# The sum B11 + B12 of one weight matrix stands further down in VectorE's program

## The reference

```python
x_not = jnp.take(field_vectors, not_idx, axis=1)
t = jnp.tanh(jax.nn.relu(x_not @ Wn1 + bn1) @ Wn2 + bn2)
iv = field_vectors.at[:, not_idx, :].set(t)

def pair_fuse(pairs, W1, b1, W2, b2):
    v = jnp.concatenate([jnp.take(iv, pairs[:, 0], axis=1), jnp.take(iv, pairs[:, 1], axis=1)], axis=-1)
    return jax.nn.relu(v @ W1 + b1) @ W2 + b2
and_out = pair_fuse(and_pairs, Wa1, ba1, Wa2, ba2)
or_out = pair_fuse(or_pairs, Wo1, bo1, Wo2, bo2)
...
h = jnp.concatenate([z, dense_ctx], axis=1)
h = jnp.maximum(h @ W_top1 + b_top1, 0.0)
h = jnp.maximum(h @ W_top2 + b_top2, 0.0)
y = h @ W_top3
```

## Time and profile before

| | us |
|---|---|
| three runs | 534.53, 537.44, 537.46 |
| median | 537.44 |
| the profiled execution | 535.43 |
| its span | 533.6 |
| TensorE busy in the span | 527.0 |
| VectorE, ScalarE, GpSimd busy | 360.9, 250.4, 241.6 |

### The profile page before, as it was taken

How to read it: one execution, slowest core, us unless ns; L and a number is a source line. 1 busy time by engine, 2 the same in 40 slices (tenths; PEclk the granted TensorE clock), 3 DMA queues, 4 the chain that set the end, 5 groups by cost and what they waited for, 6 DMA issues and landing times.

```text
span 533.6 us, 6218 instructions
## 1 busy us (share of the span) xinstructions
PE 527.0 (99%) x2385; PEld 437.0 (82%) x2385; DVE 360.9 (68%) x366; ACT 250.4 (47%) x305; POOL 241.6 (45%) x202
## 2 busy tenths in 40 slices
PE   8989999999999999999999999999999999999998
PEld 6978888888888888888888888888888888888885
DVE  5358899999785786787549788533332883678732
ACT  3675575747366453634446545232244433134343
POOL 5038876589856503551563258888566000000000
PEclk9999999999999999999999999999999999999999
DMA  7779665755895655678395358245999223241000
GB/s 261 248 198 215 127 214 165 180 152 130 198 216 157 120 119 152 110 130 160 95 269 161 117 150 273 79 120 114 242 262 232 97 89 110 83 123 48 0 0 1
DMA packets 39536, 78.95 MB, mean 148 GB/s; under 512 B 7281, under 2 KB 7537, under 8 KB 39506
## 3 DMA queue, kind: packets, MB, share of 16 engines
q0 software_dynamic: 19552, 40.93, 34.7%
q1 hardware_dynamic: 19522, 37.51, 23.0%
q10 hardware_dynamic: 432, 0.11, 0.1%
HBM read 86.90 MB, written 0.00 MB: 163 GB/s over the span
## 4 chain that ended last, share of the span: by engine, by line
PE 93%; DMA 3%; POOL 1%; DVE 1%; issue 1%; ACT 0%; SPq 0%
PE PS L1117 92%; DMA XR<-table,rows 2%; DMA WR<-weights 1%; PE PS L1288 1%; POOL XR L496 1%; POOL XR L500 1%; DMA XR<-ints 0%; PE PS L1295 0%; DVE WR L866 0%; DVE WO L846 0%; PE PS L1125 0%; PE PS L1193 0%; ACT XR L789 0%; ACT XR L792 0%; SPq L465 0%
## 5 line engine op out<-in xcount | busy, mean ns | idle before, releaser
L1117 PE MATMUL PS<-XO,WO 128*128 128x512 f32 (+1 forms) x2256 | 503.4, 385 | 1.7 <-DVE WO L846 1.7
L1117 PEld LDWEIGHTS PS<-XO,WO 128*128 128x128 f32 x2256 | 417.1, 188 | 86.2 <-DVE WO L846 1.9
L631 ACT ACTIVATE WO<-WR 128x1024 fp32r<-128x1024 f32 x93 | 98.6, 1060 | 238.8 <-PE PS L1117 233.7
L846 DVE TENSOR_TENSOR WO<-WR,WO 128x1024 fp32r<-128x1024 f32 x93 | 113.9, 1225 | 125.7 <-ACT WO L631 122.0
L510 POOL DMA_INDIRECT XR<-table,rows x96 | 124.5, 1297 | 94.6 <-PE PS L1117 61.3
L660 ACT ACTIVATE XO<-XR 128x1024 fp32r<-128x1024 f32 (+1 forms) x76 | 79.2, 1045 | 2.5 <-DVE XR L986 2.5
L924 DVE TENSOR_TENSOR XO<-XR,XO 128x1024 fp32r<-128x1024 f32 x60 | 73.0, 1218 | 0.7 <-ACT XO L660 0.7
L599 POOL DMA_INDIRECT XR<-table,rows_rest x32 | 53.8, 1681 | 15.4 <-issue 9.8
L526 POOL DMA_DIRECT2D WR<-weights x30 | 38.2, 1542 | 45.9 <-DVE WO L846 20.6
L937 DVE STREAM_TRANSPOSE XR<-XR 128x1024 f32<-128x1024 f32 x24 | 51.6, 2150 | 0.0
L986 DVE TENSOR_TENSOR XR<-XR 128x1024 f32<-128x1024 f32 (+1 forms) x32 | 38.7, 1218 | 1.8 <-ACT XR L729 1.8
(11 more groups left out here) (74 smaller groups left out, 119.5 us busy)
## 6 DMA issues: line engine op xcount, KB each, us to landing
WR<-weights SPq DMA_DIRECT2D x71, 512.0 KB
WR<-weights POOLq DMA_DIRECT2D x30, 512.0 KB, 6.9
XR<-XR POOLq DMA_DIRECT2D x32, 64.0 KB, 5.2
XR<-table,rows POOLq DMA_INDIRECT x104, 8.3
XR<-table,rows_rest POOLq DMA_INDIRECT x32
XR<-dense_t SPq DMA_DIRECT2D x3, 32.0 KB, 3.8
XR<-w_dense SPq DMA_DIRECT2D x3, 32.0 KB, 3.6
XR<-ints SPq DMA_DIRECT2D x1, 84.0 KB, 2.1
```

Source lines behind the costliest of these rows:

```text
L631: nc.scalar.activation(WO[:, n % 2, 0, :], WR[:, slot, :], ACT.Copy).then_inc(w_hi, 1)
L846: V_.tensor_tensor(WO[:, n % 2, 1, :], WR[:, raw_slot(n), :], WO[:, n % 2, 0, :].bitcast(FP32), ALU.subtract).then_inc(w_lo, 1)
L1117: mm = nc.tensor.matmul(PS[:, bank, cols], WO_t[:, slot, ws, i, k, :], XO[:, x0 + k, xs, cols], start=first and k == 0 and n == 0, stop=la ...
```

## The change

The two additions that make B11 + B12 (each with its wait for the landing of a half of B12) leave their place ahead of VectorE's loop and stand inside it, at t = 3. So they come behind `split_w(2)`, which stands at t = 2, and ahead of `split_w(3)` at t = 4. Nothing else is changed, on any engine.

```diff
@@ -861,10 +861,6 @@
                 x0_lo(h, 2)
                 x0_lo(h, 3)
 
-            for i in range(2):
-                dve.wait_ge(raw_in[2 + i], 16)
-                V_.tensor_tensor(WR[:, i, :], WR[:, i, :], WR[:, 2 + i, :], ALU.add).then_inc(t1_sum, 1)
-
             def rest_setup():
 
                 V_.tensor_reduce(in_pair, hot[:, 2 * F:].rearrange("p (s f) -> p f s", f=F), AX.X, ALU.max)
@@ -1082,7 +1078,12 @@
                     for at, key, i in SUMS:
                         if at == t:
                             operand_sum(*key, i)
-                    if t == 9:
+                    if t == 3:
+
+                        for i in range(2):
+                            dve.wait_ge(raw_in[2 + i], 16)
+                            V_.tensor_tensor(WR[:, i, :], WR[:, i, :], WR[:, 2 + i, :], ALU.add).then_inc(t1_sum, 1)
+                    elif t == 9:
                         rest_setup()
                     elif t == 16:
                         pair_setup()
```

## The result

The changed kernel takes 533.25 us (median of 12 runs, 532.89 to 533.58), the kernel before 537.36 (12 runs, 534.39 to 539.0). The medians differ by 4.1 us, 0.76%. The ratio of the runs is 0.9933, with a 95% interval of 0.9917 to 0.9950, which is 3.6 us (2.7 to 4.5). Either way two things are to be explained, not one: the gain is about twice the 1.96 us of the forecast, and the spread of the runs fell from 4.6 us to 0.7.

The account below looks back on a forecast made before the run. TensorE was taken to bound the kernel, with one hole before t = 4. Its single term of 1.96 us, off the 537.44 us median, gave 535.5 us; the range was 532.5 to 537.5 us.

Parts of the forecast that it names:

- The cause: At P2's start (t = 4), TensorE waits for VectorE's low part of weight piece 2, held behind two sums awaiting their transfers.
- The term of 1.96 us: TensorE's hole before t = 4: the start moves from 32.13 to 30.17 us, taking 1.96 us off the span.
- The median ... is 2.0 above it, so I forecast 537.44 - 1.96.: Whole kernel: the 1.96 us gain is subtracted from the median of three runs, 537.44, giving 535.5 us.
- What the landing does: B12's raw pieces: transfers of 6.2 to 8.6 us set the hole's size, so the gain's bounds are 1.7 and 4.1 us.
- More: Rival: landings in common runs are as slow as the 8.6 us transfer row, giving 533.3 to 534.5 us; chance 12%.
- the slow row: Profile row for a 512 KB transfer of GpSimd's adds, 8.6 us; it would make the hole before 2.15 us larger.
- One for one: Hole before t = 4: the term depends one for one on when the raw pieces land.
- The absorbed 2.9 us: VectorE's sums in the new order: up to 2.9 us of landing lateness is absorbed.
- The near gates: Gates after t = 4: x1_keep(1, 2) is 1.0 us early for t = 6, ScalarE is free for split_w(4) 0.45 us early.
- Both are 4.0 us early or more.: GpSimd's adds for Q6 and P4 don't move but land 4.0 us or more before they are read.
- given back: Rival: VectorE's full stretch at 60 to 120 us or GpSimd's unmoved stream makes TensorE wait; 537.0 to 537.4 us; chance 12%.
- Slower: Rival: a late ScalarE high part of piece 2 delays the sums, and TensorE stops at t = 6; up to 539.8 us; chance 3%.

Follow-up runs that it names:

- e2: The changed kernel with SyncE issuing both halves of B12 one step of ScalarE later: 532.84 us, ratio 0.9934 to the kernel before.
- e4: The kernel before, VectorE's order kept, with SyncE loading both halves of B12 early, ahead of piece 3 and without their two waits: 532.77 us, ratio 0.9935.
- e7: The kernel before, unchanged, run again for a second trace: 536.86 us.
- e9: The changed kernel, unchanged, run again: 532.92 us (532.67 to 533.03).
- e8: The kernel before, unchanged, run again for a third trace: 538.04 us.
- e1: The kernel before, VectorE's order kept, with SyncE issuing both halves of B12 one step of ScalarE later: 539.23 us, 0.44% above the kernel before.
- e3: Against the changed kernel, the first addition goes back ahead of VectorE's loop, so only the second is moved: 534.29 us, ratio 0.9958 to the kernel before.
- e10: The changed kernel with GpSimd's two adds for P4 issued ahead of two of the gathers that stood before them: 532.80 us.
- e6: e1 with twelve matmuls more on TensorE, result never read, in the hole ahead of P2: 536.60 us (535.75 to 538.18).
- e5: The kernel before with six matmuls more on TensorE, result never read, between the last transposes and entry 1: 535.77 us, ratio 0.9984.

## Why the prediction was right, and where it fell short

The measured 533.25 us lies in the range (532.5 to 537.5), within 1% as 96% had it, and on the side that was forecast. The likeliest number, 535.5, was 2.3 us too high: the gain is 4.1 us between the medians and not 1.96.

- *The cause.* Right. L846 behind the two additions closed TensorE's gate, and e2 and e4 show that the landing behind them was all of it: each takes away the dependence on it, one by order and one by an earlier load, and both end at 532.8.
- *The term of 1.96 us.* Right for the execution that it was read from: 2.78 us before, 0.82 after. It is mis-sized for the median, in two parts. In e7, near the median of before, t = 4 starts at 32.00, and in e9 at 29.47: 2.53 us. The quarter behind it takes 1.58 us longer. The sum, 4.1 us, is the difference of their spans (535.0 and 530.9) and that of the medians.
- *"The median ... is 2.0 above it, so I forecast 537.44 - 1.96."* This is the step that failed. The distance of 2.0 us between the profiled execution and the median was carried over as if it were the same in both kernels. It was the effect itself: in most runs of before (36 of 50) the clock falls behind the hole, and these are the runs of 536.49 us and more.
- *What the landing does.* The bounds of 1.7 and 4.1 us came from the duration of the transfer. The duration was 6.42 us in e7 and 6.25 in e8, as in the first trace. What varied was when TensorE arrived (28.43 and 28.56 us for its last transposes, against 29.35) and when the loads were issued (23.14 and 24.52 us for the last piece, against 23.25). No transfer of B12 in the chains of these traces took 8.6 us; the longest is e1's 7.53. The upper bound held by luck, since the clock wasn't in it. "One for one" is wrong once the clock falls: e3 saved 2.9 us for a change that is worth 1.3.
- *The rival "More", 533.3 to 534.5, 12%.* Its time came true, just beyond its end, but not its mechanism, landings as slow as the 8.6 us of the slow row: the transfers of e7 and e8 were as long as in the first trace, and the rest was TensorE's earlier arrival, later issues and the clock. Its spread of runs was the right hint, and it was worth more than 12%.
- *The absorbed 2.9 us.* Right as far as tried. Against TensorE's last transposes the sums began 0.90 us early in the first trace (28.45, 29.35), 0.99 us late in e2 (29.72, 28.73) and 1.46 us late in e9 (30.11, 28.65). So up to 2.4 us of it were taken, and nothing was lost.
- *The near gates.* Right. x1_keep(1, 2) starts at 34.26 without waiting for TensorE, straight behind the copies (forecast 34.91, less the 0.53 us of the earlier start, so 34.38). split_w(4) starts at 36.39 after 0.54 us of idle time (forecast 0.45).
- *"Both are 4.0 us early or more."* Wrong for P4. The row gave one landing of 6.2 us for two issues, and I used it for both, and compared with piece 10 alone; piece 11 was the late one. So 0.6 us of "given back" came true in the profiled execution, by GpSimd's stream and not by VectorE's full stretch, which moved along with TensorE. I can't give its cost in the median: with the adds moved (e10) the median is 0.12 us lower, within the spread of both.
- *Slower.* Nothing of it was seen; the high part of piece 2 was not late (its low part runs at 26.49, early).

## What to carry to other kernels

A short hole of the bounding engine is to be priced from several executions and not from the one that was profiled: where the profiled time lies 2 us below the median, ask what the others do in that hole before subtracting anything; the list of their granted clocks says it without another trace. On an in-order engine, work that waits for a transfer belongs behind the work whose data is already there; the gain isn't the wait of one trace but the independence from the landing, and the spread of the runs shows it first (4.6 us against 0.7). When a stream of one engine isn't moved and the demand is, check each of its pieces, the last of a group above all.

## What the runs showed of the hardware

- TensorE's granted clock fell to the 1.2 GHz level behind listed waits of 2.50, 3.59 and 5.13 us (e7, e8, e1), and stayed full behind waits of 1.71, 1.47, 1.39 and 0.92 us (before, e3, e6, e5). In e7 and e8 it fell within the first us after TensorE had gone on, in e1 inside the wait. A fall cost 1.58 us twice and 2.4 us once, in one quarter of 12 matmuls. A mean clock of 0.997 or 0.994 over the span is all that it leaves in the list of cores, and that number alone parts the 50 runs of before into those up to 536.26 us and those from 536.49 us.
- Twelve matmuls whose result nobody reads, put into such a hole, made a kernel 2.6 us faster (536.60 us in e6 against 539.23 in e1), with the clock full in all of its runs.
- The start of TensorE's real work varied by up to 0.9 us between executions of the same kernel (first transposes of the second group at 10.97, 11.04 and 11.89 us), while the transfer of B12's second half (512 KB) took 6.25 to 6.45 us in the three traces of before; with the later issue it took 6.54 us (e6) and 7.53 us (e1).
